# Attention and gated feed-forward on one core: new tables of preferences and margins for the planner that orders the queues

## What is computed

```python
qkv = x @ w_attn + b_attn;  q, k, v = split(qkv)
attn = softmax(q @ k.T / sqrt(C) + causal_mask)
x = layernorm(x + (attn @ v) @ w_proj + b_proj)
scores = x @ w_router                       # one number a row
_, top_idx = top_k(scores, int(L * 0.75))   # in each sequence
out = x.at[top_idx].set(gelu(x[top_idx] @ w_block))
x = layernorm(x + out)
```

## Time and profile before

| | |
|---|---|
| median of 3 runs | 954.26 us (953.89 to 955.04) |
| span of the profiled execution | 953.7 us |
| its time as a run | not among the three; their lowest is 0.2 us over this span, their median 0.6 us |
| PE busy | 931.6 us, 98% |
| DVE busy | 785.4 us, 82% |
| ACT busy | 633.7 us, 66% |
| POOL busy | 305.0 us, 32% |

### The profile page before, as it was taken

The page is one execution under the profiler, slowest core; times in us unless marked ns, Lnnn a source line. Parts: engine busy times, 40 slices in busy tenths (PEclk is TensorE's granted clock), DMA queues, the critical chain, the costliest instruction groups (busy, mean ns, idle before and its releaser), DMA issues.

```text
span 953.7 us, 15684 instructions
## 1 busy us (share of the span) xinstructions
PE 931.6 (98%) x5030; PEld 798.6 (84%) x5030; DVE 785.4 (82%) x1497; ACT 633.7 (66%) x1011; POOL 305.0 (32%) x460
## 2 busy tenths in 40 slices
PE   9999999999999999999999999999999999999992
PEld 6889998888888888888888999888888888888871
DVE  5898887866994896589879999998699799659977
ACT  3576665864774594479565866677578569547994
POOL 3541141242230335333325361452022244301243
PEclk9999999999999999999999999999999999999996
DMA  6644344344353355468634534346777734437934
GB/s 193 206 123 154 104 144 122 103 144 152 101 185 113 111 155 175 146 205 263 195 104 149 189 93 142 130 123 207 234 238 226 242 113 134 150 105 238 323 124 177
DMA packets 89044, 155.84 MB, mean 163 GB/s; under 512 B 8442, under 2 KB 18300, under 8 KB 88964
## 3 DMA queue, kind: packets, MB, share of 16 engines
q1 hardware_dynamic: 88964, 154.85, 51.0%
HBM read 114.96 MB, written 39.86 MB: 162 GB/s over the span
## 4 chain that ended last, share of the span: by engine, by line
PE 85%; DVE 7%; ACT 4%; issue 2%; DMA 1%; DVEq 0%; SPq 0%; ACTq 0%
PE sbank L587 37%; PE fbank L587 12%; PE obank L1236 9%; PE obank L1237 9%; PE obank L1238 9%; PE obank L1232 2%; PE obank L1230 2%; PE obank L1231 2%; DVE ring L1147 1%; ACT parts L1161 1%; DVE ring_lo L1166 1%; ACT ring L1154 1%; DMA ring<-xt 1%; DVE tail L2037 1%; PE mbank L1134 1%
## 5 line engine op out<-in xcount | busy, mean ns | idle before, releaser
L587 PE MATMUL sbank<-qT,xT 128*128 128x512 f32 (+2 forms) x1728 | 406.6, 377 | 1.1 <-ACT ring L1021 1.0
L587 PEld LDWEIGHTS sbank<-qT,xT 128*128 128x128 f32 x1728 | 306.4, 188 | 54.9 <-ACT ring L1021 1.1
L1021 ACT COPY ring<-sbank 128x512 f32<-128x512 f32 (+3 forms) x286 | 157.2, 553 | 178.3 <-PE sbank L587 125.1
L1166 DVE TENSOR_TENSOR ring_lo<-ring,parts 128x1024 fp32r<-128x1024 f32 (+4 forms) x174 | 181.1, 1050 | 32.2 <-ACT parts L1161 31.4
L1161 ACT CAST parts<-ring 128x1024 fp32r<-128x1024 f32 (+4 forms) x174 | 145.0, 843 | 48.1 <-PE obank L1238 34.1
L1070 DVE TENSOR_TENSOR runmax<-ring,runmax 128x1024 f32<-128x1024 f32 x84 | 107.1, 1274 | 69.0 <-ACT ring L1021 68.1
L1147 DVE TENSOR_TENSOR ring<-ring,mbank 128x1024 f32<-128x1024 f32 (+4 forms) x174 | 157.0, 955 | 5.6 <-PE mbank L1134 5.3
L1236 PE MATMUL obank<-ring_lo,vs 128*128 128x512 f32 (+3 forms) x416 | 158.9, 382 | 0.2 <-DVE ring_lo L1166 0.2
L1238 PE MATMUL obank<-parts,vs 128*128 128x512 f32 (+3 forms) x416 | 157.4, 378 | 0.0
L1237 PE MATMUL obank<-parts,vs 128*128 128x512 f32 (+3 forms) x416 | 157.4, 378 | 0.0
L1154 ACT ACTIVATE ring<-ring 128x1024 f32<-128x1024 f32 (+4 forms) x174 | 142.2, 852 | 9.7 <-DVE ring L1147 9.5
(11 more groups left out here) (268 smaller groups left out, 1371.4 us busy)
## 6 DMA issues: line engine op xcount, KB each, us to landing
vs<-v_scratch SPq DMA_DIRECT2D x288, 256.0 KB, 2.9
v_scratch<-vnew SPq DMA_DIRECT2D x30, 512.0 KB, 3.5
out<-tail SPq DMA_DIRECT2D x32, 256.0 KB, 2.6
xres<-x SPq DMA_DIRECT2D x15, 512.0 KB, 3.9
x_scratch<-xres SPq DMA_DIRECT2D x14, 512.0 KB, 3.9
y_scratch<-yb SPq DMA_DIRECT2D x14, 512.0 KB, 3.0
tail<-x_scratch SPq DMA_DIRECT2D x28, 256.0 KB, 3.6
tail<-y_scratch SPq DMA_DIRECT2D x28, 256.0 KB, 4.3
```

Source lines behind the costliest of these rows:

```text
L587: mm = eng.matmul(o, lhs(lh, k), rhs(rh, k), start=n == 0, stop=n == len(todo) - 1)
L1021: act.copy(slot(n)[:, c0:], sbank[n % NSS][:, c0:]).then_inc(a_copy, 1)
L1166: dve.tensor_tensor(slots_lo(ns, c0), slots(ns, c0), f32(hi_of(u)), ALU.subtract).then_inc(v_lo, 1)
```

## The change

Only the numbers of the four tables `PREFER_US`, `MARGIN_US`, `BEFORE_LAST_US` and `LAST_US` change; they were chosen by following the planned queues with every operation's duration from the trace. No stream, operation, wait, buffer or transfer is added or removed, and the planner itself (`COSTS`, `planned`) is the same. The preferences are some four times as large as before. A few entries:

```diff
-PREFER_US = {"final result": 2182, "scores copy": 1183, "prepare keys": 1153, "final pick": 1052,
+PREFER_US = {"attention_out aggr": 8537, "last chain": 6643, "late": 5251, "final result": 4708,
...
-MARGIN_US = {"late": 8, "project xhi": 8, "prepare bias": 8, "final_roots": 8, "attention_out store": 8,
+MARGIN_US = {"late": 16.1, "final sums": 10.5, "project xhi": 9.1, "prepare bias": 9, "ffn stats": 6.7,
```

More of the change, by code:

```diff
@@ new lines @@
+MARGIN_US = {"late": 16.1, "final sums": 10.5, "project xhi": 9.1, "prepare bias": 9, "ffn stats": 6.7,
+             "final pick": 5.5, "final_roots": 5.5, "attention_out residual": 5, "project xlo": 4.8, "ffn rows": 4.7,
+             "final scale": 3.6, "attention_out istd": 3.3, "final own": 3.3, "prepare keys": 3, "ffn scale": 2.5,
+             "attention_out router": 2.3, "ffn sums": 2.2, "attention_out norm": 2, "attention_out store": 2,
+             "project load": 1.6, "final result": 1.5, "project vlo": 1.5, "row_max reduce": 1.5, "search": 1.5,
+             "softmax exp": 1.5, "attention_out score": 1.3, "ffn gelu": 1.3, "ffn store": 1, "final choose": 1,
+             "last": 1, "last router": 1, "search first": 1, "attention_out stats": 0.8, "last chain": 0.7,
+             "late load": 0.7, "project vstore": 0.7, "attention_out aggr": 0.6, "attention_out load": 0.6,
+             "attention_out ot": 0.6, "bias columns": 0.6, "ffn flo": 0.6, "final load": 0.6, "out": 0.6, "proj": 0.6,
+             "values load": 0.6, "values": 0.5, "attention_out evac": 0.3, "ffn add": 0.3, "final_roots own": 0.3,
+             "project vhi": 0.3, "scores": 0.3, "scores hide": 0.3}
```

84 lines of the change are left out of this document (44 added, 40 removed).

## The result

The change is slower by about 0.2 to 0.3%. Its six runs took 956.89 us (955.11 to 958.11) beside 954.84 (953.89 to 955.04): a ratio of 1.0023, 95% interval 1.0013 to 1.0033. Eleven more took 957.80 (957.13 to 958.45), 1.0028 (1.0019 to 1.0038). The forecast was 953.6 us and no measurable change, with a range of 951.5 to 956.5 us for 8 in 10.

A forecast was written before the change was run, and what follows sets the result against it. PE's queue of products bounds the kernel, with 22.1 us idle. -1.17 + 0.1 - 0.44 + 0.3 + 0.2 + 0.6 = -0.4 us, and -0.2 us for longer real gaps, from 954.26 give 953.6 us; range 951.5 to 956.5.

The forecast's parts named there:

- The end: Last group, search and picks: late high part +0.2 us, search rounds 0, picks +0.6 us.
- second rival: Beginning wins nothing: later loads or the port lock make the projection wait 1 to 2 us; 955.1 us, chance 0.14.
- the middle: Turns between beginning and end: -0.44 us at group 14, +0.3 us at groups 10 to 12.
- The beginning: Start of the kernel: PE's waits of 1.00 and 0.17 us go, -1.17 us; +0.1 us for a new projection wait.
- the projection at 22 us: Group 1's first projection on PE: may wait for POOL's subtractions after a later load, 0.1 us, range 0 to 2.
- The baseline: Starting point of the sum: profiled span of 953.7 us taken as 0.6 us under the median of 954.26 us.
- Group 14: Two PE waits, 0.23 and 0.21 us, for low parts go as DVE's statistics move earlier: -0.44 us.
- Groups 10 to 12: PE's turns move 2.8 to 4.5 us of products nearer the last score, risking waits: +0.3 us, bounds 0 and 2.7.
- first rival: Groups 11 and 12: DVE's backlog delays the maxima and PE waits; 956.0 us, 956.5 with like waits elsewhere; chance 0.15.
- The late high part: Late feed-forward's first high part from ACT comes some 1.2 us later, search count does not wait: +0.2 us.
- The picks: One statistic and the aggregates stand between threshold and picks on DVE, shifting all 16 picks and last store: +0.6 us.
- The rounds of the search: Long product blocks move from the third to later search rounds: 0, with 0.7 us to both sides.

The follow-up runs named there:

- fill: Changed kernel plus six throwaway products in TensorE's waits in the last group, three before the second transposes, three before the late block: 956.35 us, 1.0017 of before.
- copies_first: Kernel before, with only ScalarE's first three score-bank copies moved ahead of the first cast of group 1's input: 955.16 us, 1.0002 of before.
- early: Changed order up to a planned time of 900 us, the order of the kernel before behind it: 959.60 us, 1.0046 of before.
- late_back: Changed kernel with the last two steps of the late tiles' products back between the two sets of transposes on TensorE: 956.50 us, 1.0017 of before.
- fill_one: Changed kernel plus only three throwaway products, those ahead of the second transposes: 956.91 us, 1.0021 of before.
- again: Changed kernel run once more, unaltered, against the kernel before: 957.80 us, 1.0028 of before.
- reduce_first: Changed kernel with the six throwaway products, and group 11's reduction moved ahead of two router sums and the aggregates on VectorE: 955.17 us, 1.0007 of before.
- others_only: Kernel before with TensorE's order kept, the other engines taking the changed order from 900 us on: 958.45 us, 1.0036 of before.

## Why the prediction was wrong

**The step that failed** most is "The end". It has the fact, "PE, which now has the late tiles' products ahead of the transposes" (six of the twelve stand ahead, six right behind the first set), and prices it by durations at full clock. That the clock could fall stood neither in the sum nor among the rivals. By the two traces it costs 1.9 us: the end takes 85.68 us in the execution where it fell and 83.76 where it did not. Most runs have the fall, so the median has it, and *fill* lies 1.45 us lower. Two other terms failed beside it, and the sum needs all three: the gain of the beginning, which is not there in the median (as the title of the second rival says, though not by the wait that it names), and the middle, which loses where -0.14 us was forecast.

**The beginning, -1.17 + 0.1 us.** As an account of the two profiled executions it is right: the third tile's scores start at 16.37 us without a wait, and 29.29 became 28.27. But 1.00 us is the price of one landing. Over many runs the old beginning is worth about the same as the new one, by the estimate above and by *copies_first*. The customer that I feared, the projection at 22 us, did not wait: the load landed at 17.1 us, not 18.8. Another one did. The timeline of the change, DVE, POOL and PE:

```profile
26.08 0.91 DVE L1127 TENSOR_TENSOR mcol<-mcol,row_const 128x4 f32<-128x4 f32 x1
27.02 1.20 DVE L1129 TENSOR_TENSOR mcol<-mcol,row_const 128x4 f32<-128x4 f32 x1
...
25.68 2.52 POOL L895 TENSOR_TENSOR xT<-ring,xT 128x512 fp32r<-128x512 f32 x2 [4.38 <-ACT xT L877]
...
28.27 0.65 PE L1135 MATMUL mbank<-ident,mcol 128*128 128x128 f32 x4 [0.43 <-DVE mcol L1129]
```

Two steps that take 0.16 us by the median of their 16 take 2.1 us beside POOL's subtractions. The prediction weighed the exclusive lock on the ports that DVE and POOL share (the Trainium skill, SBUF — State Buffer, on SBUF's two separate sides) and left it out of the sum, since it looked only at the maxima; by these rows the trace agrees with the rule, at the reduction instead.

**The baseline.** I took the profiled execution, 953.7 us of span, to be 0.6 us under the median. By the medians of every kernel a run's time is 1.7 to 1.8 us over its span. The profiled execution was then one of about 955.4 us, above the median, and so a gain worked out from its waits need not be one of the median.

**Group 14, -0.44 us.** Right in size in the first trace, but not safe. Over PE's pace (see the next paragraph) the two waits were 0.39 and 0.38 us. Both are gone, and a smaller one, 0.35 us, stands 4 us later, right after DVE's part of the same projection (L938) ends at 787.77 us:

```profile
787.87 3.00 PE L588 MATMUL sbank<-qT,xT 128*128 128x512 f32 x12 [0.19 <-issue]
```

And in *early*, which has the same queues there, the maximum does come late for PE, which the prediction had held possible only if DVE had no room:

```profile
772.43 0.66 PE L1112 MATMUL mbank<-ident,runmax 128*128 128x128 f32 x4 [0.85 <-DVE runmax L1066]
```

DVE's step L1066 took 1.77 us there, from 770.61 on, beside POOL's subtractions from 770.51 on; in the first trace of the change it took 0.69 us and ended before them.

**Groups 10 to 12, +0.3 us.** The first rival's place, at groups 10 and 11, and not at 12; its mechanism, DVE work ahead of the maximum, in part, since at group 11 the reduction is late and not the maximum. Its size can be read from PE's pace: for every row the start of the next one less its own, less the median of that for its shape, summed over a stretch. From 480 to 600 us that is 0.7 us before and in *copies_first*, and 1.9 us in both traces of the change. In the first one the timeline at group 11's turn, DVE, POOL and PE, reads so:

```profile
566.32 1.21 DVE L1129 TENSOR_TENSOR mcol<-mcol,row_const 128x4 f32<-128x4 f32 x1
...
564.98 2.53 POOL L1675 TENSOR_TENSOR yb<-xres,yb 128x512 f32<-128x512 f32 x2
...
567.58 0.65 PE L1135 MATMUL mbank<-ident,mcol 128*128 128x128 f32 x4 [0.39 <-DVE mcol L1129]
```

Over the whole middle, 840.4 to 841.4 us in six traces with the old one and 841.6 to 842.6 in six with the new one, the change loses 0.8 us by the medians where I had -0.14.

**The late high part, +0.2 us.** Under-sized. The copy L1621 starts at 918.75 us where L1620 started at 917.87, and its customer waits 0.63 us for 0.23 in the one trace, and 1.6 and 1.7 us in *late_back* and *fill_one*. PE also waits 0.67 us at 911.03 us for values that are still being loaded (0.3 us in the second trace), a wait that before does not have and the prediction did not see. "The count does not wait for it" was true, and beside the point: PE did.

**The picks, +0.6 us.** Right for this step, but not for the end. The timeline of the change on DVE, the last step of the ties and the two that were moved:

```profile
939.29 0.20 DVE L1825 SCALAR_TENSOR_TENSOR mbank<-keyf,gteq 128x32 f32<-128x32 f32 x1
939.52 0.43 DVE L1681 BATCH_NORM_STATS2 bnst<-tail 128x6 f32<-128x256 f32 x1
939.87 0.36 DVE L1686 BATCH_NORM_AGGREGATE mv_y<-bnst 128x2 f32<-128x6 f32 x4
```

The first pick starts at 940.14, 0.65 us behind the end of the ties, and before it was 0.09 us. My remark that their customer is wanted 8.6 us later holds because they stand ahead of the picks; *early* shows the 5.3 us that the chain needs. Yet the ties themselves end 0.3 us earlier, counted from the last row of L588, so the first pick comes only 0.25 us later and the whole end at full clock is 0.2 us longer, where the forecast's terms make 0.8. The rounds of the search, put at 0 with 0.7 us to both sides, gave the difference back in this trace.

**The sum** by median spans, 953.0 before and 956.0 for *again*: beginning 0, middle +0.8, end +2.2 (85.7 for 83.5; 0.2 to 0.3 of it without the clock). The beginning's part is the estimate above, the others are from traces. What stays open: why the same queues meet the fall of the clock in 11 to 15 of 17 executions, by their mean clock, and not in the others; how much of the fall is PE's own order and how much ACT's later high part; and what part of the 1.2 us between *fill* and *reduce_first* is the turn itself (by PE's pace about 0.6 us).

## What to carry over

- Where TensorE's queue goes from dense products to transposes and one-column products, look at the granted clock of many runs, not of one trace; keep some dense work for that stretch, and if there is none, throwaway products in its waits are cheap: six of them kept the mean clock at 0.992 or more in 10 of 11 runs here.
- A wait for a transfer in one trace is one draw. Before a gain is taken from it, see whether the profiled execution is typical: its own time beside the median, with what lies outside the span measured.
- An order is tuned as a whole. Half of one plan beside half of another cost up to 4.9 us here, more than either plan, so such hybrids tell where to look, and single moved steps tell causes.

## What the runs showed of the hardware

- The clock fell to its lower level at 918 us although PE's longest wait there was 0.72 us; before the fall PE was busy for 1.28 us of 2.00 with transposes, a short count and products of one column. It also fell in the beginning, behind waits of 1.28, 1.46 and 2.18 us, and in *fill_one* within a wait of 1.69 us. It did not fall at waits of 1.6 us in the traces of *late_back* and *others_only*.
- Two-operand DVE steps of 4 columns took 0.70 to 1.25 us beside POOL's sums or subtractions, and 0.16 us at the median.
- The same load of 512 KB, issued at 8.2 to 8.9 us, let its cast start at 14.38 us in one execution and at 16.46 us in another.
